# Signals per head between first-pass scores and row maxima, and a later place for head 1 of four steps

## The reference

```
x = x + xattn(layernorm(x), ctx, Wq, Wkv, Wout)     # 16 heads of 32, causal, softmax
x = x + ffn(layernorm(x), router, experts)          # top 2 of 8 per token and column
```

```
scores = einsum('bhqd,bhkd->bhqk', qh, kh) / sqrt(32)
attn   = softmax(where(causal, scores, min))
out    = einsum('bhqk,bhkd->bhqd', attn, vh)
```

## Time and profile before

| | |
|---|---|
| median of 3 runs | 2113.99 us (2113.83 to 2118.13) |
| profiled execution | 2117.69 us, span 2116.0 us |
| TensorE busy | 2005.6 us, 95% |
| VectorE busy | 1509.3 us, 71% |
| ScalarE busy | 1006.0 us, 48% |
| GpSimd busy | 850.7 us, 40% |
| TensorE busy, 0 to 700 us (attention) | 605.18 us |
| TensorE busy, 700 to 2116 us | 1400.46 us |
| mean granted clock, 0 to 700 us | 0.93 |
| mean granted clock, 700 to 2116 us | 1.00 |

### The profile page before, as it was taken

The page is one execution under the profiler, slowest core; times in us unless marked ns, Lnnn a source line. Parts: engine busy times, 40 slices in busy tenths (PEclk is TensorE's granted clock), DMA queues, the critical chain, the costliest instruction groups (busy, mean ns, idle before and its releaser), DMA issues.

```text
span 2116.0 us, 31087 instructions
## 1 busy us (share of the span) xinstructions
PE 2005.6 (95%) x9822; PEld 1513.4 (72%) x9872; DVE 1509.3 (71%) x3300; ACT 1006.0 (48%) x2030; POOL 850.7 (40%) x985
## 2 busy tenths in 40 slices
PE   3889999999997899999999999999999999999999
PEld 2556666656654577777777777778888888888887
DVE  4677777777677657777777777757877878878533
ACT  1454454454443436776767776743433334433300
POOL 2566767666666434344344344301311113211100
PEclk8789999999998999999999999999999999999999
DMA  5345445445445445455454454462232222322110
GB/s 154 90 102 141 114 116 140 119 117 134 108 111 180 148 186 198 154 184 186 166 204 178 175 184 169 179 254 94 93 105 80 74 94 84 115 79 75 59 40 30
DMA packets 99220, 275.85 MB, mean 130 GB/s; under 512 B 13435, under 2 KB 14480, under 8 KB 95030
## 3 DMA queue, kind: packets, MB, share of 16 engines
q1 hardware_dynamic: 94518, 216.16, 32.1%
q10 hardware_dynamic: 4608, 58.72, 8.1%
HBM read 131.67 MB, written 92.27 MB: 106 GB/s over the span
## 4 chain that ended last, share of the span: by engine, by line
PE 80%; DVE 13%; DMA 2%; issue 2%; POOL 1%; SPq 1%; ACT 1%; DVEq 0%; POOLq 0%; ACTq 0%
PE pair L262 21%; PE pair L264 20%; PE pair L263 20%; DVE pair L1250 5%; DVE o_sb L1271 4%; PE ps L647 3%; PE pair L606 3%; PE pair L839 2%; PE ps L262 2%; PE pair L634 2%; PE ps L263 1%; PE ps L264 1%; DVE nmax L1250 1%; PE ps L667 1%; DVE qk L1234 1%
## 5 line engine op out<-in xcount | busy, mean ns | idle before, releaser
L262 PE MATMUL pair<-w_h,hT 128*128 128x512 f32 x1920 | 796.6, 415 | 3.3 <-DVE xb L1578 1.7
L264 PE MATMUL pair<-w_h,hT 128*128 128x512 f32 x1920 | 751.0, 391 | 0.0
L263 PE MATMUL pair<-w_l,hT 128*128 128x512 f32 x1920 | 747.0, 389 | 0.0
L1769 POOL TENSOR_TENSOR logits<-logits,second 128x512 f32<-128x512 f32 x224 | 298.2, 1365 | 606.9 <-DVE second L1457 606.5
L264 PEld LDWEIGHTS pair<-w_h,hT 128*128 128x128 f32 x1920 | 360.2, 188 | 80.2
L263 PEld LDWEIGHTS pair<-w_l,hT 128*128 128x128 f32 x1920 | 361.2, 188 | 74.6
L262 PEld LDWEIGHTS pair<-w_h,hT 128*128 128x128 f32 x1920 | 362.8, 189 | 71.0 <-issue 2.1
L1250 DVE CUSTOM_DVE_ANT_0 pair<-pair,future 128x256 f32<-128x256 f32 (+3 forms) x512 | 240.0, 510 | 132.7 <-PE pair L606 132.7
L1578 DVE SCALAR_TENSOR_TENSOR xb<-pair,c_now,xb 128x512 f32<-128x512 f32 x256 | 191.8, 749 | 188.5 <-PE pair L264 182.0
L992 ACT ACTIVATE pT<-pair,zero 128x1024 f32<-128x1024 f32 (+3 forms) x256 | 202.8, 793 | 254.2 <-PE pair L634 250.7
L606 PE MATMUL pair<-qk_st 96*128 96x256 f32 (+3 forms) x512 | 144.0, 364 | 47.7 <-DVE nmax L1250 43.7
(11 more groups left out here) (161 smaller groups left out, 2811.3 us busy)
## 6 DMA issues: line engine op xcount, KB each, us to landing
logits<-lg_all ACTq DMA_DIRECT2D x32, 1792.0 KB, 7.7
qk_st<-qk SPq DMA_DIRECT2D x384, 128.0 KB, 2.3
lg_all<-ev_a SPq DMA_DIRECT2D x32, 768.0 KB, 5.7
lg_all<-ev_b SPq DMA_DIRECT2D x32, 768.0 KB, 3.2
xb<-x SPq DMA_DIRECT2D x64, 256.0 KB, 3.1
hT_all<-hT SPq DMA_DIRECT2D x32, 512.0 KB, 3.6
hT<-hT_all SPq DMA_DIRECT2D x32, 512.0 KB, 3.7
xt<-in_x SPq DMA_DIRECT2D x8, 1024.0 KB, 5.5
```

What stands on the lines that cost most here:

```text
L262: pe.matmul(dst, lh, rh, start=start, stop=False)
L263: pe.matmul(dst, lh, rl, start=False, stop=False)
L264: return pe.matmul(dst, ll, rh, start=False, stop=stop)
L1769: pool.tensor_tensor(logits[t % 2][:, e - 1, :], logits[t % 2][:, e - 1, :], second[:], ALU.subtract)\
```

## The change

Both semaphores are now raised once for each head: `scores` by each matmul, `negmax` by each maximum. TensorE waits before each head's matmul for the maximum of the same head one step before (`2 * u - 1 + j`), and VectorE waits before each head's maximum for that head's matmul (`2 * u + 1 + j`). The end count in `turn_maxima` is doubled.

For steps 0 to 3 (`LATE`), the matmul of head 1 moves: it is issued at the next position, directly behind the second-pass scores there, and ahead of that position's other work. Steps 4 to 7 keep both heads in one place. Ahead of the loop, step 1 of group 1 issues only its head 0; its head 1 comes at position 0 of the first group. VectorE's order is unchanged, and no matmul and no maximum is added or left out.

```diff
--- before.py
+++ after.py
@@ -267,6 +267,8 @@
             k = v + LEAD
             return 1 + k // UNITS, k % UNITS
+
+        LATE = 4
         def block_of(v):
@@ -590,26 +592,25 @@
                 if c == KC - 1:
                     mm.then_inc(s["wo_mm"], 1)
-            def scores(n, c, v):
+            def scores(n, c, v, heads=(0, 1)):
                 u = n * UNITS + v
                 i, pair = block_of(v), v % 2
                 w = (i + 1) * P
-                if v < 2:
+                if v < 2 and 0 in heads:
                     pe.wait_ge(s[f"stacked{pair}"], (n + 1) * (16 * STACK_DMAS))
-
-                if some(u):
-                    pe.wait_ge(s["negmax"], u)
-                for j in range(2):
+                for j in heads:
                     hh = 2 * pair + j
-                    mm = pe.matmul(s_ps[:, j, 0:w], qk_st[c][0:STACK, 0, hh, i * P:w], qk_st[c][0:STACK, 1, hh, 0:w],
-                                   start=True, stop=True)
-                mm.then_inc(s["scores"], 1)
+
+                    if some(2 * u - 1):
+                        pe.wait_ge(s["negmax"], 2 * u - 1 + j)
+                    pe.matmul(s_ps[:, j, 0:w], qk_st[c][0:STACK, 0, hh, i * P:w], qk_st[c][0:STACK, 1, hh, 0:w],
+                              start=True, stop=True).then_inc(s["scores"], 1)
             def turn_maxima(n, c):
-                pe.wait_ge(s["negmax"], (n + 1) * UNITS)
+                pe.wait_ge(s["negmax"], (n + 1) * UNITS * 2)
                 if some(n - 1):
                     pe.wait_ge(s["o_ok"], n - 1)
@@ -720,7 +721,7 @@
             freed("K", 1)
             keys(2, 0, 0)
             for v in range(LEAD):
-                scores(1, 1, v)
+                scores(1, 1, v, (0, 1) if v < LEAD - 1 else (0,))
             pe.wait_ge(s["st_ones"], KC)
             pe.wait_ge(s["w_hi"], 3)
             pe.wait_ge(s["w_lo"], 3)
@@ -753,6 +754,9 @@
                             turn_maxima(n + 1, c + 1)
                         final = last and c == KC - 1
                         shifted_scores(n, c, v, final)
+                        g, vv = target(c, v - 1)
+                        if vv < LATE and (more or c + g < KC):
+                            scores(n + g, (c + g) % KC, vv, (1,))
                         if c == 1 and v == 0 and out:
                             project(v)
                         if c == 0 and v in VALUE:
@@ -778,7 +782,7 @@
                             project(v)
                         g, vv = target(c, v)
                         if more or c + g < KC:
-                            scores(n + g, (c + g) % KC, vv)
+                            scores(n + g, (c + g) % KC, vv, (0,) if vv < LATE else (0, 1))
                         if v == KEY and ahead:
                             take(key_bank(c), "K", n + AHEAD)
                             keys((c + AHEAD) % KC, b if c == 0 else b + 1, key_bank(c))
@@ -1240,16 +1244,15 @@
                 u = n * UNITS + v
                 i, pair = block_of(v), v % 2
-                dve.wait_ge(s["scores"], u + 1)
                 if v == 0 and some(n - 1):
                     dve.wait_ge(s["turned"], n - 1)
                 for j in range(2):
                     at = (2 * pair + j) * QB + i
+                    dve.wait_ge(s["scores"], 2 * u + 1 + j)
                     row = s_ps[:, j, 0:(i + 1) * P]
-                    op = dve.tensor_tensor_reduce(row, row, future[:, S - (i + 1) * P:S], -1.0, -MASKED, ALU.add, ALU.min,
-                                                  accum_out=nmax[:, c % 2, at:at + 1])
-                op.then_inc(s["negmax"], 1)
+                    dve.tensor_tensor_reduce(row, row, future[:, S - (i + 1) * P:S], -1.0, -MASKED, ALU.add, ALU.min,
+                                             accum_out=nmax[:, c % 2, at:at + 1]).then_inc(s["negmax"], 1)
             def lo_shift(n):
```

## The result

The changed kernel takes 2102.47 us (median of 6 runs, 2099.44 to 2105.11), the kernel before 2113.91 in as many: ratio 0.9947 [0.9932, 0.9963], a gain of 11.4 us. The forecast was 2093 in a range of 2084 to 2108. Direction and range held, but only about half of the 21.1 us came. The profiled execution took 2104.04 (span 2102.3), 13.7 less than that of before.

The account below looks back on a forecast made before the run. TensorE sets the pace, but not alone: both heads share one signal each way with VectorE. Gains 5.1 + 0.6 + 3.5 + 11.6 + 0.3 = 21.1 us take the profiled 2117.69 to 2096.6; median forecast 2093, range 2084 to 2108.

Parts of the forecast that it names:

- Startup: Group 0 of batch 0, eight steps: VectorE's idle falls from 6.9 to 1.8 us, gain 5.1 us.
- c = 3: Column block 3, a group without values or projection: step 3's maxima come earlier on VectorE, gain 0.43 us a batch.
- The stall of 0.54: Sign: TensorE's 0.54 before scores 2 in c = 3 goes; L634 waits about 0.3 us on ACT instead.
- c = 0: Column block 0, one group a batch: 0.39 us at its entry, and step 3's head 0 signalled 0.17 earlier.
- c = 2: Column block 2, one group a batch: step 3's head 0 gains, limited by the DMA rows; 0.15 us taken.
- c = 1: Column block 1, one group a batch: TensorE's stalls before scores 1 and 2 go, gain 0.8 us.
- rival C: Half-clock stretches after c = 3 change: 2076 us if gone in seven batches, 2105 if each 3.4 longer; chance 0.07.
- Batch 0: First batch, no projection, all its groups like c = 3 with a half-clock stretch: gain 3.5 us.
- Last batch: Gains 0.56 us in c = 0, later gains swallowed by waits for rows behind router weights: 0.3 us.
- A: Rival: second-pass scores (L634) wait for exponentials or rows everywhere, not only in c = 3; 2103 us, chance 0.19.
- B: Rival: head 1, queued behind second-pass scores in steps 0 to 3, starves VectorE; slower, 2121 us, chance 0.07.
- D: Rival: nothing, the gains are taken back by waits priced at zero; 2113 to 2117 us, chance 0.07.

Follow-up runs that it names:

- e1: The changed kernel with LATE = 0: signals per head, both heads of every step in one place; 2095.38 us, ratio 0.9916 to before.
- e12: The changed kernel with second-pass scores of steps 4 and 5 in c = 3 repeated to fill TensorE's stalls; 2087.49 us, ratio 0.9879.
- e13: The kernel before with the same repeated second-pass scores in c = 3 as e12; 2101.74 us, ratio 0.9950.
- e5: The changed kernel with late head 1 put ahead of the second-pass scores, not behind; 2089.27 us, ratio 0.9885 to before.
- e9: e1 without the TensorE waits that another wait implies; 2095.38 us, ratio 0.9913 to before.
- e2: The kernel before with per-head signals only in the startup and the two lead steps; 2105.95 us, ratio 0.9968.
- e8: The kernel before with both semaphores raised once per head, all waits still for both heads; 2114.01 us, ratio 1.0004.
- e10: The kernel before without the TensorE waits that another wait implies; 2113.26 us, ratio 0.9997.
- e14: e5 without the TensorE waits that another wait implies (lean waits); 2080.87 us, ratio 0.9851 to before.
- e15: e5 with the repeated second-pass scores of e12; 2082.95 us, ratio 0.9860 to before.

## Why the prediction was right or wrong

*Startup: right.* VectorE's idle fell to 1.2 (forecast 1.8) and the first turning came 5.1 earlier (forecast 5.1).

*c = 3: right, with one size off.* The timeline of TensorE in the change, batch 3; the turning is at 344.82, so 6.43 and 9.25 us lie between it and the scores of steps 2 and 3, against 7.02 and 9.45 before, where the turning is at 355.00:

```profile
351.25 0.44 PE L608 MATMUL pair<-qk_st 96*128 96x384 f32 x1
351.79 0.74 PE L635 MATMUL pair<-qk_st 98*128 98x512 f32 x2
352.37 0.34 PE L608 MATMUL pair<-qk_st 96*128 96x384 f32 x1
...
354.07 0.44 PE L608 MATMUL pair<-qk_st 96*128 96x384 f32 x1
```

VectorE, the same stretch, to be held against the earlier trace rows:

```profile
352.75 0.56 DVE L1254 CUSTOM_DVE_ANT_0 pair<-pair,future 128x384 f32<-128x384 f32 x1 [0.39 <-PE pair L608]
...
354.55 0.57 DVE L1254 CUSTOM_DVE_ANT_0 pair<-pair,future 128x384 f32<-128x384 f32 x1 [1.18 <-PE pair L608]
```

The stall of 0.54 is gone, and L635 waits about 0.1 for the exponential where 0.3 was forecast. Step 3's maxima start 9.73 us behind the turning instead of 10.11: 0.38, and the group is 0.36 shorter in this batch (18.22 to 17.86). The rule that step 3's gain is the group's gain holds. But e1, with head 1 in its old place, has 0.34 of it (17.89): the shift behind the second-pass scores, by which this group's forecast was worked out, was not needed for it.

*c = 0 and c = 2* came near: 0.46 of 0.56 and 0.18 of 0.15.

*c = 1: the step that failed in the groups.* The prediction said of the waits behind the two stalls: "TensorE reaches them at 319.92 and 322.06: neither is late by more than 0.05", and took 0.8. The next wait was late by more. It is that of the projection for the turned tokens' lower part (L1229), and the row above shows the stall: 0.33 us. Counted from the turning, the load comes at 6.44 before and 6.49 after, so nothing of the first stall's 0.49 was won. VectorE's chain (transposes, upper part, lower part, among the maxima) sets that point, and three waits taken one at a time stand behind it. The trace of before already had the 0.32 us: the first lower part ends at 319.91, the load comes at 320.23, and only the second-pass matmuls, which run to 320.40, hid it:

```profile
319.78 0.62 PE L634 MATMUL pair<-qk_st 98*128 98x512 f32 x2
320.23 0.19 PEld L262 LDWEIGHTS ps<-wo_h,oT_h 128*128 128x128 f32 x1 [0.25 <-issue]
320.26 0.47 PE L262 MATMUL ps<-wo_h,oT_h 128*128 128x512 f32 x1
```

I had weighed the dependency, but not that TensorE would now arrive ahead of it and pay for each wait. What is left is 0.35, of which the 0.28 of scores 2 is likely the most; that split is not shown.

*The clock: the term that was set to zero.* The prediction held the half-clock stretches to be fixed ("The stalls of steps 5 to 7, just ahead of it, stay, so I expect them to stay") and gave rival C 7 in 100. Its own test names it: "if the half-clock stretches change in length: then the clock, not the loop, made the time". They did, though the stalls themselves got shorter (1.40 us in three after the change against 2.16 in five before). In the steady batches of before a stretch is 3.4 or 6.8 us long, nearly all at the entry of c = 0. The change has one of 10.2 at 362.5, and two of 3.4 us inside c = 2, where before has one. A c = 0 group with the long stretch takes 21.19 against 16.8, a c = 2 group with the extra one 21.2 against 19.62. The sum: the six batches give 9.2 us at full clock (e12 against e13) and gave 5.2; the missing 4.0 is the clock's. Low time there is equal (32.8 and 34.0), but it costs 0.46 us each in the change (15.0 / 32.8, against e12) and 0.32 before (11.0 / 34.0, against e13). A likely reason, not shown by a run: with less waiting, more of each stretch is TensorE's own work.

*Batch 0: 3.5 forecast, none had, and the clock is again the likely reason.* At like low time the loop's new signals do gain: e5 and e9 need 76.6 us each for this batch with 15.1 and 15.2 us of low time, e2, which waits for both heads in the loop, 78.4 with 13.5. The order of the change has 25.2 us of low time there (29.7 in e12) where kernels with the waits of before have 18.0 to 18.8 (e8, e10, e13; 34.2 in the one profile of before). The change has stretches of 10.2 us at 86.0 and 106.5, which in e5 are 6.8 and 3.4 long. Windows of the change:

```profile
82.00:86.00 4.00, 2.63 (x12) 1.60 (x11) 4.00 (x12) 1.98 (x3) 3.83 (x5) 1.00 0.73 253
86.00:96.20 10.20, 9.84 (x40) 5.28 (x41) 6.49 (x23) 2.33 (x5) 7.49 (x19) 0.50 0.24 56
96.20:106.50 10.30, 9.10 (x58) 5.84 (x56) 9.25 (x30) 7.96 (x11) 7.33 (x12) 1.00 0.44 102
106.50:117.00 10.50, 9.86 (x40) 5.37 (x41) 4.50 (x14) 2.36 (x5) 4.46 (x7) 0.51 0.34 78
```

and of e5:

```profile
82.00:86.00 4.00, 3.13 (x14) 1.80 (x12) 4.00 (x15) 2.63 (x4) 3.92 (x4) 1.00 0.82 269
86.00:96.20 10.20, 9.40 (x45) 5.15 (x45) 8.05 (x27) 2.69 (x5) 7.75 (x19) 0.67 0.17 39
96.20:106.50 10.30, 8.52 (x55) 5.38 (x54) 9.02 (x31) 7.56 (x10) 8.46 (x13) 1.00 0.52 120
106.50:117.00 10.50, 10.50 (x71) 5.50 (x72) 5.18 (x18) 4.83 (x8) 6.12 (x11) 0.84 0.41 95
```

Ahead of the first fall TensorE was busy 2.63 of 4 us in the change and 3.13 in e5, but ahead of the second 9.10 of 10.3 and 8.52. So the busy share before a fall does not sort the two. Why this order lets the clock fall longer stays open; that it does is in the comparison of the change with e5, whose undisturbed groups c = 1 to 3 are equal in length within 0.07 us.

*Last batch.* 0.3 forecast; it took 64.7 us instead of 63.3, with 34.1 us of low time from its first group to 720 us against 22.6 before.

*The rivals.* A named nearly the measured time (2103) for a reason that did not occur: L635's weight loads wait 3.7 us for exponentials from 60 to 680 us. B, head 1 starving VectorE, did not occur in that form: groups with head 1 late and in place are equally long. C is what took the gain back, at places I had not looked at. Its faster end has a slip: 20 us under the forecast of 2093 is 2073, not 2076. D fell. With the chances as they stood, luck has a part in the range's holding: the time is nearest to A, whose mechanism did not occur. On increments, e8 settles what the prediction left between two values. The Trainium skill (TensorE: Matmul & The Clock Gate, "The cost: per-tile semaphore tail") describes a serial cost of 26.3 ns per increment for tiles that finish together, an estimated 6.7 us here. The 0.9 [-1.5, 3.0] of e8 lies below it: the matmuls here, which follow one another, do not pay it.

*The best version.* e14, per-head signals, head 1 late but ahead of the second-pass scores, and lean waits: 2080.87 us, 0.9851 [0.9835, 0.9866]. It is 8.4 us below e5, of which its lower low time (57.3 against 76.2) makes an estimated 7.6 at 0.40; its six batches take 450.5, e5's 451.1. Against e15 (2082.95), the filled e5, no difference can be told: the two ratios overlap. The repeated matmuls on top of e14 were not tried.

## What to carry to other kernels

Price a change in two ledgers: the time between fixed points at full clock, and the time at the lower level; compare orders of equal work on the second, for here it moved the time by as much as the first. Before believing a small gain in a kernel with TensorE over 90% busy, fill its known stalls with repeated matmuls, in both versions: that shows the change by itself where the clock is held, and may be the better kernel. When a change has two parts, run each alone: here one of them bought nothing in the groups and cost 5 to 7 us in time. Where a stall is removed, write down the time at which each wait behind it is met, to 0.1 us, and count the wait instructions that stand in a row there.

## What the runs showed of the hardware

- The clock fell after c = 3's stalls, four of 0.18 to 0.79 us and 0.46 at the turning in 7 us before, while TensorE was over 90% busy over the batch. Eight repeated matmuls a batch kept it at 2.4 GHz in the six steady batches, and the kernel became 12 to 15 us shorter by doing more.
- A microsecond at the lower level cost 0.32 to 0.46 us (0.25 to 0.40 by the fitted lines), less than the 0.5 that TensorE's own work loses at half speed; where the rest hides was not tried.
- Consecutive waits on TensorE's queue took about 0.1 us each (310.408, the one that VectorE's lower part ended, then .514, .611, load at .687). Where matmuls already queued ran on meanwhile, they cost nothing that can be told (load at 320.23 in before without idle of the matmuls; e10: 0.9997 [0.9988, 1.0006]).
- 256 more semaphore increments on TensorE and on VectorE had no price that can be told (e8: 1.0004 [0.9993, 1.0014]).
- A single profile can mislead: that of before took 25.4 us for one group with 15.7 us at the lower level, where e10's took 21.1 with 4.7. A sum made against its span counts the difference as a cost of the code.
